# An attention and FP4 feed-forward layer on 8 cores: quantized weight tiles finished one tile later, and softmax reciprocals on 128 partitions

## The reference

```python
xn = layernorm(x)                      # no scale, no bias
Q, K, V = xn @ WQ, xn @ WK, xn @ WV    # 16 heads of 64
attn = softmax(causal(Q K^T / 8)) V @ WO
gate = fp4(xn) @ fp4(w_gate).T         # 1024 -> 2816
up   = fp4(xn) @ fp4(w_up).T
ffn  = fp4(silu(gate) * up) @ fp4(w_down).T
out  = x + attn + ffn
```

## Time and profile before

| | us |
|---|---|
| median of the runs (2) | 9346.0 |
| lowest, highest | 9342.1, 9349.9 |
| the profiled execution | 9332.7 |
| its span on core 6, the slowest | 9331.2 |
| spans of cores 0 to 3 | 9191.5 to 9221.9 |
| spans of cores 4 to 7 | 9240.9 to 9331.2 |

### The profile page before, as it was taken

How to read it: one execution, slowest core, us unless ns; L and a number is a source line. 1 busy time by engine, 2 the same in 40 slices (tenths; PEclk the granted TensorE clock), 3 DMA queues, 4 the chain that set the end, 5 groups by cost and what they waited for, 6 DMA issues and landing times.

```text
span 9331.2 us, 80918 instructions; the slowest of 8 cores (9191.5 to 9331.2 us)
## 1 busy us (share of the span) xinstructions
PE 5771.9 (62%) x21136; PEld 2262.4 (24%) x21136; DVE 3134.8 (34%) x5204; ACT 2404.7 (26%) x4112; POOL 2344.6 (25%) x2257
## 2 busy tenths in 40 slices
PE   0000003788578755988477747886677548884777
PEld 0000001322133322322133313221233223221333
DVE  1222335100036655000066652001366550001665
ACT  0000003255311123355111132553111134551111
POOL 0222222111223422011134421112233320112333
PEclk9999996755578866655688857555888767557888
DMA  3111111000320010000410010001311100004010
GB/s 120 40 40 40 44 54 43 14 1 1 85 92 35 34 55 21 10 1 1 150 41 34 34 52 19 1 1 46 124 37 39 52 23 10 1 1 163 28 41 34
DMA packets 143215, 387.42 MB, mean 42 GB/s; under 512 B 78208, under 2 KB 79232, under 8 KB 134016
## 3 DMA queue, kind: packets, MB, share of 16 engines
q1 hardware_dynamic: 142784, 382.25, 12.5%
HBM read 288.36 MB, written 93.32 MB: 41 GB/s over the span
## 4 chain that ended last, share of the span: by engine, by line
PE 38%; DVE 24%; POOL 11%; DMA 9%; issue 8%; ACT 8%; DVEq 1%; SPq 1%; POOLq 0%; ACTq 0%
PE ps_c L592 8%; PE ps_a L566 5%; POOL heap L585 5%; DVE heap L235 4%; DVE heap L226 4%; PE ps_b L566 4%; DVE heap L257 3%; PE ps_a L737 3%; DVE heap L229 3%; POOL heap L245 3%; PE ps_a L532 3%; PE ps_b L532 3%; POOL heap L247 3%; PE ps_a L679 2%; DVE heap L757 2%
## 5 line engine op out<-in xcount | busy, mean ns | idle before, releaser
L245 POOL TENSOR_TENSOR heap<-heap 128x512 f32<-128x512 f32 (+3 forms) x564 | 861.6, 1528 | 3958.1 <-DVE heap L241 3693.5
L592 PE MATMUL ps_c<-heap 128*65 128x512 bf16 (+3 forms) x2560 | 1174.7, 558 | 296.1 <-ACT heap L578 225.2
L603 DVE CAST heap<-ps_c 64x512 bf16<-64x512 f32 x256 | 174.9, 683 | 2843.2 <-PE ps_c L592 2843.2
L585 POOL TENSOR_TENSOR heap<-heap,tri 128x128 bf16<-128x128 bf16 x1024 | 436.2, 426 | 2579.9 <-ACT heap L578 2470.2
L578 ACT ACTIVATE heap<-ps_a 128x512 bf16<-128x512 f32 (+1 forms) x1280 | 667.7, 573 | 603.4 <-PE ps_a L566 596.8
L247 POOL TENSOR_TENSOR heap<-heap 128x512 f32<-128x512 f32 (+3 forms) x564 | 765.3, 1357 | 82.3 <-POOL heap L245 2.2
L787 PE MATMUL ps_c<-heap 128*128 128x512 bf16 x2816 | 727.8, 426 | 5.0 <-ACT heap L821 5.0
L311 PE MATMUL ps_t<-idn,heap 128*128 128x128 bf16 x352 | 44.5, 306 | 982.0 <-DVE heap L257 982.0
L566 PE MATMUL ps_a<-heap 64*128 64x512 bf16 (+1 forms) x1280 | 631.0, 595 | 0.0
L592 PEld LDWEIGHTS ps_c<-heap 128*65 128x65 bf16 x2560 | 325.8, 130 | 1255.1 <-issue 1248.4
L257 DVE TENSOR_TENSOR heap<-heap 128x512 bf16<-128x512 f32 (+3 forms) x564 | 413.5, 733 | 603.4 <-POOL heap L247 602.9
(11 more groups left out here) (73 smaller groups left out, 6222.4 us busy)
## 6 DMA issues: line engine op xcount, KB each, us to landing
heap<-x SPq DMA_DIRECT2D x128, 512.0 KB, 3.7
heap<-rz_d SPq DMA_DIRECT2D x64, 512.0 KB, 6.4
attn_scr<-heap SPq DMA_DIRECT2D x64, 512.0 KB, 2.6
heap<-attn_scr SPq DMA_DIRECT2D x64, 512.0 KB, 4.5
out<-heap SPq DMA_DIRECT2D x64, 512.0 KB, 2.6
heap<-wg_d SPq DMA_DIRECT2D x4, 5632.0 KB, 20.1
heap<-wu_d SPq DMA_DIRECT2D x4, 5632.0 KB, 33.5
heap<-wd_d SPq DMA_DIRECT2D x4, 5632.0 KB, 16.4
```

The lines of the kernel that those rows point to most:

```text
L245: P.emit("gpsimd", lambda e: e.tensor_tensor(u, u, M, op=ALU.add), waits=[(s_ve, ve_m), (s_po, s_po.n)], inc=(s_po, 1))
L585: P.emit("gpsimd", lambda e, eb=eb: e.tensor_tensor(eb[:, 0:128], eb[:, 0:128], tri[:], op=ALU.mult), waits=[(s_ac, ac_exp), (s_po, s_po.n ...
L592: p_=p_, s_=s_, vst=vst, jm=jmax: e.matmul(pv[0:65, off:off + n], vst[:, j, p_ * 2 + s_, 0:65], eb[:, 0:n], start=(j == 0), stop=(j == jm ...
```

## The change

It has two parts.

**Staging.** In the loops over w_gate, w_up and w_down, `quant_deq` and all that follows it (transposes, ACT's copy, the store) are moved into functions, `flush_gu` and `flush_wd`. An iteration now emits the load and `quant_pre` of its own tile and then the flush of the tile before; a last flush follows each loop. The buffers are those of before.

**Softmax sums.** Each head's row goes straight to DRAM (`rz_d`), not to `zbuf`. After the last head, `zbuf` is loaded from `rz_d` as 128 partitions x 256 columns, the reciprocal is taken there, and it is written back to `rz_d` in the same shape. The three weight loads (wo_d, wg_d, wu_d) are moved from behind the broadcasts to ahead of the load of `zbuf`.

The core of the diff:

```diff
@@ staging, w_gate and w_up (w_down alike)
-                ve_q = quant_deq(tok, stgb, D, extra_pe_wait=stgb_rd[wp])
-                stg_rd[wp] = ve_q
...
+        def flush_gu(pend):
+            ic, wp, stgb, tok, wout = pend
+            ve_q = quant_deq(tok, stgb, D, extra_pe_wait=stgb_rd[wp])
+            stg_rd[wp] = max(stg_rd[wp], ve_q)
...
+        pend = None
         for win, wout in ((wg_in, wg_d), (wu_in, wu_d)):
             for ic in range(NI):
...
                 P.wait("vector", [(s_w, s_w.n)])
                 tok = quant_pre(stg, W_U[wp], W_M[wp], W_QS[wp], D)
+                if pend is not None:
+                    flush_gu(pend)
+                pend = (ic, wp, stgb, tok, wout)
+        flush_gu(pend)
@@ softmax sums
-            zbuf = vf(ZBUF, S, parts=16)
+            zbuf = vf(ZBUF, S // 8, parts=128)
...
-                    out=zbuf[h:h + 1, :], in_=ztmp[0:1, :]),
+                    out=rz_d[h:h + 1, :], in_=ztmp[0:1, :]),
...
             pe_attn_done = s_pe.n
 
+            wo_sb = vb(WOT, NCD * D).rearrange("p (c n) -> p c n", n=D)
+            P.emit("sync", lambda e, wo_sb=wo_sb: e.dma_start(out=wo_sb, in_=wo_d[:]),
+                   waits=[(s_pe, pe_attn_done)], inc=(s_w, 16))
...
+            P.emit("sync", lambda e, wgq=wgq: e.dma_start(out=wgq, in_=wg_d[:]),
+                   waits=[(s_ws, ws_stageW), (s_w, s_w.n)], inc=(s_w, 16))
+            P.emit("sync", lambda e, wuq=wuq: e.dma_start(out=wuq, in_=wu_d[:]),
+                   inc=(s_w, 16))
...
+            P.emit("sync", lambda e, zbuf=zbuf: e.dma_start(
+                out=zbuf[:, :], in_=rz_d.rearrange("h (a c) -> (h a) c", a=8)),
+                waits=[(s_zg[0], ws_zg2[0]), (s_zg[1], ws_zg2[1])], inc=(s_ws, 16))
+            ws_zld = s_ws.n
             P.emit("vector", lambda e, zbuf=zbuf: e.reciprocal(zbuf[:, :], zbuf[:, :]),
-                   waits=[(s_zg[0], ws_zg2[0]), (s_zg[1], ws_zg2[1]), (s_ve, s_ve.n)],
-                   inc=(s_ve, 1))
+                   waits=[(s_ws, ws_zld), (s_ve, s_ve.n)], inc=(s_ve, 1))
```

More of the change, by code:

```diff
@@ L279, in build_core_program @@
         stgb_rd = [0, 0]
-        st2_rd = 0
+        st2_rd = [0]
         for win, wout in ((wqt_in, wq_d), (wkt_in, wk_d), (wvt_in, wv_d), (wot_in, wo_d)):
@@ L296, in build_core_program @@
         P.wait("vector", [(s_ws, ws_attnW)])
+        def flush_gu(pend):
+            ic, wp, stgb, tok, wout = pend
+            ve_q = quant_deq(tok, stgb, D, extra_pe_wait=stgb_rd[wp])
+            stg_rd[wp] = max(stg_rd[wp], ve_q)
+            for c in range(NCD):
+                P.emit("tensor", lambda e, stgb=stgb, c=c: e.transpose(
+                    ps_t[:, c * 128:(c + 1) * 128], stgb[:, c * 128:(c + 1) * 128], idn[:]),
+                    waits=([(s_ve, ve_q), (s_ac, s_ac.n), (s_po, po_const)] if c == 0 else []),
+                    inc=((s_pe, 1) if c == NCD - 1 else None))
+            stgb_rd[wp] = s_pe.n
+            stg2 = vb(W_ST2, D)
+            P.emit("scalar", lambda e, stg2=stg2: e.copy(stg2, ps_t[:]),
+                   waits=[(s_pe, s_pe.n)] + ([(s_ws, st2_rd[0])] if st2_rd[0] else []),
+                   inc=(s_ac, 1))
+            P.emit("sync", lambda e, wout=wout, ic=ic, stg2=stg2: e.dma_start(
+                out=wout[:, :, ic * 128:(ic + 1) * 128],
+                in_=stg2.rearrange("p (c i) -> p c i", i=128)),
+                waits=[(s_ac, s_ac.n)], inc=(s_ws, 16))
+            st2_rd[0] = s_ws.n
+        pend = None
         for win, wout in ((wg_in, wg_d), (wu_in, wu_d)):
@@ L307, in build_core_program, with flush_wd @@
                 tok = quant_pre(stg, W_U[wp], W_M[wp], W_QS[wp], D)
-                ve_q = quant_deq(tok, stgb, D, extra_pe_wait=stgb_rd[wp])
-                stg_rd[wp] = ve_q
[L310 to L334, removed]
+                if pend is not None:
+                    flush_gu(pend)
+                pend = (ic, wp, stgb, tok, wout)
+        flush_gu(pend)
+        def flush_wd(pend):
+            c, wp, stgb, tok = pend
             ve_q = quant_deq(tok, stgb, I, extra_pe_wait=stgb_rd[wp])
-            stg_rd[wp] = ve_q
+            stg_rd[wp] = max(stg_rd[wp], ve_q)
             done = 0
@@ L347, in build_core_program @@
                 P.emit("scalar", lambda e, stg2=stg2, g=g: e.copy(stg2, ps_t[:, 0:g * 128]),
-                       waits=[(s_pe, s_pe.n)] + ([(s_ws, st2_rd)] if st2_rd else []),
+                       waits=[(s_pe, s_pe.n)] + ([(s_ws, st2_rd[0])] if st2_rd[0] else []),
                        inc=(s_ac, 1))
@@ L353, in build_core_program @@
                     waits=[(s_ac, s_ac.n)], inc=(s_ws, 16))
-                st2_rd = s_ws.n
+                st2_rd[0] = s_ws.n
                 done += g
             stgb_rd[wp] = s_pe.n
+        pend = None
+        for c in range(NCD):
+            wp = wk_i % 2
+            wk_i += 1
+            stg, stgb = vf(W_STG[wp], I), vb(W_QBF[wp], I)
+            P.emit("sync", lambda e, c=c, stg=stg: e.dma_start(
+                out=stg, in_=wd_in[c * 128:(c + 1) * 128, :]),
+                waits=[(s_w, s_w.n), (s_ve, stg_rd[wp])], inc=(s_w, 16))
+            P.wait("vector", [(s_w, s_w.n)])
+            tok = quant_pre(stg, W_U[wp], W_M[wp], W_QS[wp], I)
+            if pend is not None:
+                flush_wd(pend)
+            pend = (c, wp, stgb, tok)
+        flush_wd(pend)
         ws_stageW = s_ws.n
@@ L614, in build_core_program @@
                     pc_rd[qc % 2] = (ve_pc, s_ac.n)
-                P.emit("sync", lambda e, h=h, ztmp=ztmp, zbuf=zbuf: e.dma_start(
-                    out=zbuf[h:h + 1, :], in_=ztmp[0:1, :]),
+                P.emit("sync", lambda e, h=h, ztmp=ztmp: e.dma_start(
+                    out=rz_d[h:h + 1, :], in_=ztmp[0:1, :]),
                     waits=[(s_ac, s_ac.n)], inc=(s_zg[h % 2], 16))
@@ L619, in build_core_program @@
             pe_attn_done = s_pe.n
+            wo_sb = vb(WOT, NCD * D).rearrange("p (c n) -> p c n", n=D)
+            P.emit("sync", lambda e, wo_sb=wo_sb: e.dma_start(out=wo_sb, in_=wo_d[:]),
+                   waits=[(s_pe, pe_attn_done)], inc=(s_w, 16))
+            w_wo_ld = s_w.n
+            wgq = vb(F_WG, NCD * I).rearrange("p (c i) -> p c i", i=I)
+            wuq = vb(F_WU, NCD * I).rearrange("p (c i) -> p c i", i=I)
+            P.emit("sync", lambda e, wgq=wgq: e.dma_start(out=wgq, in_=wg_d[:]),
+                   waits=[(s_ws, ws_stageW), (s_w, s_w.n)], inc=(s_w, 16))
+            P.emit("sync", lambda e, wuq=wuq: e.dma_start(out=wuq, in_=wu_d[:]),
+                   inc=(s_w, 16))
+            w_gu_ld = s_w.n
+            P.emit("sync", lambda e, zbuf=zbuf: e.dma_start(
+                out=zbuf[:, :], in_=rz_d.rearrange("h (a c) -> (h a) c", a=8)),
+                waits=[(s_zg[0], ws_zg2[0]), (s_zg[1], ws_zg2[1])], inc=(s_ws, 16))
+            ws_zld = s_ws.n
             P.emit("vector", lambda e, zbuf=zbuf: e.reciprocal(zbuf[:, :], zbuf[:, :]),
-                   waits=[(s_zg[0], ws_zg2[0]), (s_zg[1], ws_zg2[1]), (s_ve, s_ve.n)],
-                   inc=(s_ve, 1))
+                   waits=[(s_ws, ws_zld), (s_ve, s_ve.n)], inc=(s_ve, 1))
             ve_rz = s_ve.n
-            P.emit("sync", lambda e, zbuf=zbuf: e.dma_start(out=rz_d[:, :], in_=zbuf[:, :]),
+            P.emit("sync", lambda e, zbuf=zbuf: e.dma_start(
+                out=rz_d.rearrange("h (a c) -> (h a) c", a=8), in_=zbuf[:, :]),
                    waits=[(s_ve, ve_rz)], inc=(s_ws, 16))
@@ L651, in build_core_program @@
             po_norm = s_po.n
[L653 to L663, removed]
             ws_ot_last = 0
```

## The result

| | us |
|---|---|
| changed kernel, median of 11 runs | 8941.0 (8917.1 to 8998.9) |
| kernel before, median of 10 runs beside it | 9253.2 (9245.9 to 9349.9) |
| ratio, 95% interval | 0.9646 (0.9613 to 0.968) |
| forecast | 9041, range 8960 to 9130; as a ratio to the 9346.0 it started from, 0.9674 |
| profiled execution of the changed kernel | span 8939.4 on core 2 |

What follows compares the result with a forecast made beforehand. Bound by chains of waits between engines, none full, in staging and at the end of attention. 9332.7 - 225 - 98 + 18 = 9027.7; with the median 13.3 above the profiled execution, 9041 us, range 8960 to 9130.

Steps and rivals of the forecast that it cites:

- the base of the sum: Whole kernel: starting time, profiled execution of 9332.7 us, 13.3 us under the shown median of 9346.0.
- w_gate and w_up: Staging of these weights: POOL's two instructions leave each tile's chain of waits, saving 225 us.
- the idle time ahead of L257 less the 0.1 us that any two DVE steps keep: Staging, per-tile saving on DVE; over 44 tiles of w_gate and w_up 228.8 - 44 x 0.1 = 224 us.
- w_down: Staging of w_down's 8 tiles: idle time ahead of L257 goes, less loop ends and port cost, saving 98 us.
- The port: Staging: DVE's L257 starts ahead of POOL's L245 and pays nothing; POOL pays some 1 us, hidden (3 for w_down).
- Tile 1's six steps: Staging of w_gate and w_up: they run against POOL's two instructions and take 7.8 us instead of 5.3.
- The rival's price: Staging: POOL's L245 starts ahead of DVE's L257, which waits in every tile; 146 us, time 9187, chance 0.07.
- After attention: End of attention, four times: later first broadcast against evacuation stalls removed; +4.5 us a batch, +18 us in all.
- the delay: End of attention: the sums' load queues behind the weight loads, so the first broadcast goes 30.6 us later.
- the return of the stall: Output projection: evacuations no longer wait for stores behind large loads, giving back 20.9 us a batch.
- The two rivals about the queue: End of attention: sums slip past the weights, 8919 us, chance 0.07; or delayed without stall time back, 9125, 0.06.
- The clock rival: Attention and FFN: PE's clock falls as staging's rest shortens, giving all back; 9417 us, chance 0.03.

Runs made afterwards that it cites:

- e7: Changed kernel with an unneeded wait for L241 added to L257, DVE's last step of a staging tile; one run of 8961.0 us.
- e8: Changed kernel with L257 of each staging tile made to wait for POOL's L245 of the next tile, so POOL comes first; one run of 9142.2 us.
- e2: Softmax-sums part alone, staging as in the kernel before; 9297.8 us, ratio 1.002 to the kernel before.
- e3: Changed kernel with the loads of wg_d and wu_d put back behind the broadcasts, wo_d still first; 8902.8 us, ratio 0.9584 to the kernel before.
- e1: Staging part alone, the rest from the first batch on as in the kernel before; 8948.2 us, ratio 0.9645 to the kernel before.
- e5: Changed kernel with each staging load issued one step earlier, ahead of the store of tile i-1; 8656.0 us, ratio 0.9315 to the kernel before.

## Why the prediction was right and wrong

**The step that failed is the base of the sum.** It reads: "The median shown, 9346.0, is 13.3 above that execution, and all changes are on every core's path, so the forecast is 9041." The changes are on every core's path, but the base was not that of a usual execution. The next 8 runs beside the changed kernel have a median of 9250.3, and of the 28 runs of the kernel before that followed the first two, one took over 9342. The trace that I used hinted at it: cores 0 to 3 had spans up to 9222 us, cores 4 to 7 up to 9331, with the same work; I took the longest as the kernel's time. With 9250 in place of 9346 the same sum gives 9250 - 305 = 8945, 4 us from the median. That it comes so near is partly luck: by the table the gain was 325 us, 20 more than forecast, 10 of them in staging and 10 in the sums part. The range was built on the doubts about the change, and had hardly any room for a wrong base.

**w_gate and w_up: 225 forecast, 233 measured** (core 4: from 166.8 to 1010.8 before, from 166.7 to 777.8 after). The term that was mis-sized is "the idle time ahead of L257 less the 0.1 us that any two DVE steps keep". L257 keeps no such gap: without a wait for L241 it starts 0.08 us ahead of that instruction's recorded end. That is 0.18 us in 42 tiles, 8 us, and e7 gives it back step by step. The row was there: in the earlier trace rows L257 starts 0.29 us ahead of a POOL instruction that the same L241 released.

**w_down: 98 forecast, 99 measured** on the same core (from its first load to the first of x, 357.7 us before, 258.4 after).

**The port.** Right: L257 unchanged at 1.22 us (no tile on any core shows a lost race), POOL's L245 0.8 us longer and hidden. Tile 1's six steps take 7.5 us instead of 5.2, near the forecast 7.8. The rival's price, 146 us, was somewhat low (170 in e8). What kept it away is a lead of 0.3 us; in e7, with 0.1, it came true in one tile.

**After attention.** The mechanism was right: the delay, the end of tile 0 about 1 us behind POOL, the return of the stall. The term that was too large is the delay, 30.6 us against 28.2 in the mean of the trace (31.1 in the batch shown), and about as much is missing in the total: +4.5 a batch forecast, some +2 measured. Such a difference is near the limit of what the runs resolve. The two rivals about the queue are out by e2 and e3.

**The clock rival** fell with e1: staging is 332 us shorter on core 4 of the traces, and the whole kernel 333. e5 shortens staging by another 291 us (mean of the cores) and the kernel by 294. The mean clock at the higher level does fall, from 0.745 to 0.736, but only because the stretch granted 1.00 is shorter: (0.745 x 9229 - 333) / 8896 gives 0.735.

## What to carry to other kernels

Software pipelining that moves only the last steps of an item behind the next item's first steps frees exactly the engine that sat between them; look next at what still stands in line (here the load behind the store on the same queue, worth another 294 us). On a queue that lands loads in order, as this one did, a small transfer that something waits for goes ahead of bulk loads, and bulk loads go in pieces between the small ones. Before a time is forecast, compare the cores of both dies in the profile: the absolute time may be off by more than the change is uncertain.

## What was not expected of the hardware

- A DVE instruction that waits for nothing on its own engine starts 0.08 us ahead of the recorded end of the one before it; a semaphore wait on that one costs 0.19 us. A lead of 0.10 us was enough for DVE to get the port; 0.25 us behind POOL's instruction, it waited until that one had ended.
- At the end of a POOL instruction a DVE instruction that it releases can overtake POOL's own next one, by 0.04 us in e8, and keeps the port for its whole 1.23 us.
- L229, with 0.2 us of work on 64 values per partition, waits for the POOL instruction that runs just as the wide ones do (0.83 us in e5), while L226 beside the same instruction keeps its 1.22 us.
